# An attention and expert block on one core: extra steps spread over 24 score units, row maxima split after their transpose

## What is computed

```python
A1 = jnp.einsum('bhqd,bhkd->bhqk', Q1, K1) * scaling
A2 = jnp.einsum('bhqd,bhkd->bhqk', Q2, K2) * scaling
...
attn = jax.nn.softmax(A1, -1) - lam * jax.nn.softmax(A2, -1)
O = jnp.einsum('bhqk,bhkd->bhqd', attn, V)
rms = jnp.sqrt(jnp.mean(O * O, -1, keepdims=True) + EPS)
O = O / rms * rms_scale * (1.0 - LAMBDA_INIT)
...
logits = jnp.einsum('bth,eh->bte', x, router_w) + router_b
topv, topi = jax.lax.top_k(logits, TOP_K)
```

## Time and profile before

| | us |
|---|---|
| median of 3 runs | 1679.91 |
| lowest and highest | 1677.23, 1682.10 |
| the profiled execution | 1678.91 |
| its span | 1677.1 |

### The profile page before, as it was taken

The page is one execution under the profiler, slowest core; times in us unless marked ns, Lnnn a source line. Parts: engine busy times, 40 slices in busy tenths (PEclk is TensorE's granted clock), DMA queues, the critical chain, the costliest instruction groups (busy, mean ns, idle before and its releaser), DMA issues. The chain is left out here.

```text
span 1677.1 us, 44178 instructions
## 1 busy us (share of the span) xinstructions
PE 1340.8 (80%) x14048; PEld 940.4 (56%) x14049; DVE 1228.7 (73%) x3090; ACT 859.4 (51%) x1918; POOL 857.3 (51%) x1283
## 2 busy tenths in 40 slices
PE   1578888888888888888888888885199999999960
PEld 0345555555555555555555555553178888888850
DVE  3467887888888888888888888876756666666647
ACT  1156667666766676667666766664123333333320
POOL 0135566666666666666666666665323333333334
PEclk9999989998999899989998999896589999999985
DMA  5453444344434443444344434410111111111129
GB/s 203 99 111 76 112 109 101 86 111 109 105 85 108 112 105 84 111 111 105 83 111 111 106 83 108 105 39 17 43 44 44 44 44 46 43 44 45 44 76 296
DMA packets 182624, 151.73 MB, mean 90 GB/s; under 512 B 29555, under 2 KB 165369, under 8 KB 182068
## 3 DMA queue, kind: packets, MB, share of 16 engines
q1 hardware_dynamic: 165124, 122.11, 30.2%
q0 software_dynamic: 8448, 16.93, 3.3%
q10 hardware_dynamic: 8880, 10.49, 1.8%
HBM read 88.26 MB, written 60.51 MB: 89 GB/s over the span
## 5 line engine op out<-in xcount | busy, mean ns | idle before, releaser
L1190 DVE TENSOR_REDUCE mx<-p_max 128x2 f32<-128x512 f32 (+1 forms) x768 | 504.9, 685 | 198.3 <-PE p_max L816 188.9
L1009 ACT ACTIVATE probs<-p_exp 128x512 f32<-128x512 f32 x768 | 440.4, 601 | 239.7 <-PE p_exp L837 150.9
L1430 POOL TENSOR_SCALAR_AFFINE_SELECT probs<-probs 128x256 f32<-128x256 f32 (+1 forms) x768 | 366.3, 486 | 344.6 <-ACT probs L1009 333.3
L866 PE MATMUL p_out<-probs,v 128*32 128x256 f32 (+1 forms) x4096 | 253.3, 371 | 42.1 <-ACT ot L1000 35.7
L659 POOL DMA_INDIRECT pair_out<-on,v x136 | 133.7, 983 | 282.4 <-ACT on L569 274.6
L808 PE MATMUL p_max<-kt,qt 50*128 50x256 bf16 x1024 | 199.3, 293 | 35.6 <-ACT probs L1009 19.0
L866 PEld LDWEIGHTS p_out<-probs,v 128*32 128x32 f32 x4096 | 124.0, 119 | 145.2 <-POOL probs L1430 67.9
L837 PE MATMUL p_exp<-qt,kt 52*128 52x256 bf16 x1024 | 205.2, 289 | 0.0
L816 PE MATMUL p_max<-tri,ids 64*128 64x128 bf16 (+1 forms) x768 | 188.7, 253 | 0.0
L633 DVE TENSOR_TENSOR ot<-ot,p_max 128x512 f32<-128x512 f32 x136 | 93.5, 688 | 123.6 <-PE p_max L520 105.0
L816 PE MATMUL p_max<-tri,idb 64*128 64x128 bf16 (+1 forms) x768 | 172.3, 252 | 0.0
(11 more groups left out here) (174 smaller groups left out, 2750.5 us busy)
## 6 DMA issues: line engine op xcount, KB each, us to landing
qt<-q_parts SPq DMA_DIRECT2D x128, 192.0 KB
q_parts<-part_h SPq DMA_DIRECT2D x96, 128.0 KB, 1.9
kt<-k_parts SPq DMA_DIRECT2D x128, 96.0 KB
v<-rows_sorted SPq DMA_DIRECT2D x136, 65.0 KB, 1.8
q_parts<-part_m SPq DMA_DIRECT2D x64, 128.0 KB, 1.9
kt<-k_parts SPq DMA_DIRECT2D x128, 64.0 KB
qt<-pair_out SPq DMA_DIRECT2D x32, 256.0 KB, 5.0
mods<-mod_rows SPq DMA_DIRECT2D x32, 192.0 KB
```

Of the source, the lines that this page charges most:

```text
L866: m = nc.tensor.matmul(p_out[32 * j:32 * j + 32, pair, SEQ - n:SEQ], v[:, b.par, tile, 2 * g + head, :], src, start=(tile == 0), stop=(til ...
L1009: nc.scalar.activation(probs[:, quad % 2, k, :], p_exp[:, n % 3, :], ACT.Exp, scale=SCALE).then_inc(exp_done.sem, 1)
L1190: V.reduce_max(mx[:, w, tile, t, heads[0]:heads[-1] + 1], p_max[:, bank, :].rearrange("p (h k) -> p h k", h=len(heads)), AX.X, negate=True ...
L1430: G.affine_select(out=blocks, in_=blocks, compare_op=ALU.is_ge, fill=zero, base=0, pattern=[[0, count], [1, P]], channel_multiplier=-1).th ...
```

## The change

Every `body` is written over the 24 score units u, one unit a step, and the extra steps are spread over them anew. On DVE each unit's extra work stands right behind that unit's maximum. Where the main pieces stand, by the number of the score unit that they follow on their engine (b: before, a: after):

| piece | engine | b | a |
|---|---|---|---|
| outputs of groups 6, 7 (bC), 0 to 5 (b2) | PE | 0, 3, 6, 9, 12, 15, 18, 21 | 0, 2, 6, 8, 12, 14, 18, 20 |
| `xn` transposed | PE | 0 | 1 |
| first, second projection | PE | 2, 5 | 3, 7 |
| `low_part` 0, 1 | POOL | 6, 9 | 7, 11 |
| `ot` to rows, bC | PE | 8, 9 | 10, 13 |
| `ot` to rows, b2 | PE | 20, 21 | 17, 19 |
| logits | PE | 11 | 11 |
| values | PE | 12 | 15 |
| maxima of half 0 to rows | PE | 14 | 13 |
| rank products (`both`) | PE | 15 | 16 |
| `o`, `osq` | POOL | 12, 14 | 15, 16 |
| Newton steps 1 and 2; 3 and 4 | DVE | 21 | 22; 23 |
| `xn`, `h2` scaled | ACT | 23 | 0, 1 of the next iteration |

The maxima go another way. `take_max` writes them in the order that the rows need; PE transposes the fp32 columns of `mx` and no longer bf16 columns; ACT copies the rows and rounds them to bf16 (the high part, `nmt[:, 0]`); and the new DVE step `low_shift` subtracts that from the fp32 rows in PSUM (the low part, `nmt[:, 1]`). `minus_max`, `nm` and the semaphore `nm_step` go. The row numbers of the experts are converted to float by a copy where a multiplication by one did it (`topf`). SP's list is the same, but for the rows that `move_max` reads.

```diff
                     for part in range(SHIFTS):
-                        row, at = HU * NT * (t * SHIFTS + part), LANE * t + SHIFT_AT + part
+                        row, at = HU * NT * t, LANE * t + SHIFT_AT + part
                         sp.dma_start(qt[at:at + 1, 2 * b.par + w, :, :].rearrange("p h (l k) -> p (h l) k", l=NT),
-                                     nmt[row:row + HU * NT, w, :]).then_inc(nm_loaded[w].sem, 16)
+                                     nmt[row:row + HU * NT, part, w, :]).then_inc(nm_loaded[w].sem, 16)
...
-                wait(pe, nm_step, b, SHIFTS * (w + 1))
+                wait(pe, max_done, b, NBANKS // 2 * (w + 1))
                 settle(pe)
-                nc.tensor.transpose(p_mix[:, 1, 0:LANE].bitcast(BF16), nm[:, w, :], idb[:]).then_inc(nm_ps.sem, 1)
+                nc.tensor.transpose(p_mix[:, 1, 0:P], mx[:, w, :], idf[:]).then_inc(nm_ps.sem, 1)
...
-                for s in range(NH):
-                    n = s + s // 2
-                    scores(b1, b2, n)
-                    if s % 2:
-                        scores(b1, b2, n + 1)
-                    if s % 2 == 0:
-                        g = s // 2 - 2
-                        if g >= 0 and active(b2):
-                            outputs(b2, g)
-                        if g < 0 and active(bC):
-                            outputs(bC, g + PAIRS)
...
+                for u in range(NBANKS):
+                    scores(b1, b2, u)
+                    if u in (0, 2) and active(bC):
+                        outputs(bC, PAIRS - 2 + u // 2)
+                    if u in (6, 8, 12, 14, 18, 20) and active(b2):
+                        outputs(b2, 2 * (u // 6 - 1) + u % 6 // 2)
+                    if u == 1 and active(b2):
                         max_to_rows(i, b2, 1, 0)
-                    if s == 2 and active(bW):
...
-                    if s == 1 and active(bA):
...
+                    if u == 3 and active(bA):
                         wait(pe, ht_ready, bA)
                         project(i, bA, 0, 1)
-                    if s == 3 and active(bW):
-                        mix_free(pe, i, 1, 2)
+                    if u == 9 and active(bW):
...
-                    if s == 3 and active(bA):
-                        project(i, bA, 1, 2)
-                    if s == 5 and active(bC):
-                        outputs_to_rows(i, bC, 1, 0, 1, 4)
-                    if s == 6 and active(bC):
-                        outputs_to_rows(i, bC, 1, 1, 0, 3)
-                    if s == 4 and active(bR):
-                        mix_free(pe, i, 1, 3)
+                    if u == 7 and active(bR):
+                        mix_free(pe, i, 1, 2)
                         wait(pe, h2_step, bR)
...
-                        mix_free(pe, i, 1, 5)
+                    if u == 7 and active(bA):
+                        project(i, bA, 1, 2)
+                    if u == 11 and active(bR):
+                        mix_free(pe, i, 1, 4)
...
-                    if s == 8 and active(bV):
-                        mix_free(pe, i, 0, 4)
+                    if u == 10 and active(bC):
+                        outputs_to_rows(i, bC, 1, 0, 0, 3)
+                    if u == 13 and active(b1):
+                        max_to_rows(i, b1, 0, 5)
+                    if u == 13 and active(bC):
+                        outputs_to_rows(i, bC, 1, 1, 0, 4)
+                    if u == 15 and active(bV):
+                        mix_free(pe, i, 0, 5)
...
-                    if s == 9 and active(b1):
-                        max_to_rows(i, b1, 0, 6)
-                    if s == 10 and active(bR):
-
-                        mix_free(pe, i, 1, 7)
+                    if u == 16 and active(bR):
+
+                        mix_free(pe, i, 1, 6)
...
-                    if s == 13 and active(b2):
-                        outputs_to_rows(i, b2, 0, 0, 0, 5)
-                    if s == 14 and active(b2):
-                        outputs_to_rows(i, b2, 0, 1, 1, 8)
+                    if u == 17 and active(b2):
+                        outputs_to_rows(i, b2, 0, 0, 0, 6)
+                    if u == 19 and active(b2):
+                        outputs_to_rows(i, b2, 0, 1, 1, 7)
...
-                nc.scalar.copy(nmt[:, w, :], p_mix[0:NM_COLS, 1, 0:LANE].bitcast(BF16)).then_inc(nmt_ready.sem, 1)
+                nc.scalar.copy(nmt[:, 0, w, :], p_mix[0:MX_COLS, 1, 0:P]).then_inc(nm_high.sem, 1)
...
-                    wait(dve, nm_step, b.plus(-1), SHIFTS * (w + 1))
-                V.reduce_max(mx[:, w, tile, t, heads[0]:heads[-1] + 1],
+                    wait(dve, nm_ps, b.plus(-1), w + 1)
+                by_head = mx[:, w, 0:MX_COLS].rearrange("p (t h a) -> p t h a", t=2, h=HU)
+                V.reduce_max(by_head[:, t, heads[0]:heads[-1] + 1, tile],
...
-            def minus_max(b, w, k):
-
-                src = mx[:, w].rearrange("p a t h -> p t h a")
-                parts = nm[:, w, 0:NM_COLS].rearrange("p (t s h a) -> p t s h a", t=2, s=SHIFTS, h=HU)
-                if k == 0:
-                    wait(dve, max_done, b, NBANKS // 2 * (w + 1))
-                    wait(dve, nm_ps, b.plus(-1), w + 1)
-                    ins = V.tensor_scalar(parts[:, :, 0], src, ones_col[:, 0:1], None, ALU.mult)
-                else:
-                    wait(dve, nm_step, b, SHIFTS * w + 1)
-                    ins = V.tensor_tensor(parts[:, :, 1], src, parts[:, :, 0], ALU.subtract)
-                ins.then_inc(nm_step.sem, 1)
+            def low_shift(b, w):
+
+                wait(dve, nm_high, b, w + 1)
+                wait(dve, nm_loaded[w], b.plus(-1))
+                V.tensor_tensor(nmt[:, 1, w, :], p_mix[0:MX_COLS, 1, 0:P], nmt[:, 0, w, :],
+                                ALU.subtract).then_inc(nmt_ready.sem, 1)
...
+                        V.tensor_copy(topf[:].rearrange("p j t -> p t j"), top8i[:, :, 0:2]).then_inc(route.sem, 1)
-                            V.tensor_scalar(topf[:].rearrange("p j t -> p t j"), top8i[:, :, 0:2], ones_col[:, 0:1], None,
-                                            ALU.mult).then_inc(route.sem, 1)
...
+                    if u == 22:
+                        inverse_roots(i, [1, 2])
+                    if u == 23:
+                        inverse_roots(i, [3, 4])
...
-                    if active(b1) and s % 2:
-                        take_max(b1, n + 1)
...
-                for s in range(NH):
+                for u in range(NBANKS):
                     if active(b2):
-                        mask_bank(b2, s + s // 2)
-                        if s % 2:
-                            mask_bank(b2, s + s // 2 + 1)
-                    if s == 5 and active(bW):
...
-                    if s in (4, 6) and active(bA):
-                        low_part(bA, (s - 4) // 2)
-                    if s == 0 and active(bR):
...
+                        mask_bank(b2, u)
+                    if u == 2 and active(bR):
...
+                    if u in (7, 11) and active(bA):
+                        low_part(bA, (u - 7) // 4)
+                    if u == 13 and active(bW):
...
-                    if s in (12, 13, 14, 15) and active(bR):
-
-                        k = s - 12
+                    for k in {21: (0,), 22: (1, 2), 23: (3,)}.get(u, ()):
+                        if not active(bR):
```

277 lines of the change are left out of this document (134 added, 143 removed).

## The result

| | before | after |
|---|---|---|
| median | 1681.01 us (4 runs) | 1719.58 us (4 runs) |
| lowest and highest | 1677.23, 1684.34 | 1706.85, 1728.98 |
| the profiled execution | 1678.91 | 1728.98 |
| its span | 1677.1 | 1727.2 |

The changed kernel takes 1.0225 times the time of before (95% interval 1.0154 to 1.0297): slower, as forecast, but by 38.6 us where 6 to 8 were forecast, and 7.6 us above the range. The profiled executions of experiments 2 and 14 were disturbed (over 1.5% above the fastest of their kernel): the ratios leave them out and I explain no time from their traces, but the medians count them (without them 1630.58 and 1670.82 us).

What follows compares the result with a forecast made beforehand. Bound: unit 0 waiting for DMA loads behind `low_part`, 17.0 + 1.7 + 15.2 = 33.9 us a period. Steady +5, early +6, last -3 on 1678.9 gave 1687 us, range 1622 to 1712.

Steps and rivals of the forecast that it cites:

- the price of the clock's fall: PE's clock drops to 0.50 before the steps leading to `low_part`, delaying it 1.7 us a steady period (0 to 3.4).
- What bounds: Claim that PE's unit 0 waits for DMA `kt<-k_parts`, a loop through DMA from `low_part`'s end; period 33.9 us.
- The end of `low_part`, 18.7 us: The second `low_part` on POOL ends 17.0 us behind unit 0 at full clock, plus 1.7 for the clock's fall.
- The string, 15.2 us: SP's stores, moves and loads from the end of the second `low_part` to the next unit 0: 15.2 us.
- Four early periods, +6: Loop's first four periods, already waiting for loads: two more units ahead of `low_part`, 1.5 us each, +6 us.
- The last iteration, -3: Last period has no loads to wait for and keeps the gain of removed PE stalls: -3 us.
- What the change takes away: DVE loses 3.4 us a period, gains about 0.6; spreading ends most PE stalls, 2 to 3 us a period.
- Full clock: Rival: loads bind but PE's clock doesn't fall before the first half; period 32.2, 1642 us (1612 to 1650); chance 0.17.
- Slower still: Rival: POOL's `o` beside DVE's `chosen` and `both` delays `low_shift`, lengthening SP's string; 35 us a period, 1717; chance 0.12.
- The spreading doesn't do what it says: Rival: PE still waits at unit 16 for `both`, up to 1.1 us under the DMA string; no separate chance.
- The engines bind: Rival: with earlier `low_part` or shorter SP string, DVE, PE and handshakes give 30 us a period, 1580 us; chance 0.09.

Runs made afterwards that it cites:

- experiment 2: Changed kernel with SP's six query stores waiting for the first `low_part` alone: 1634.42 us, 0.9718 of before.
- experiment 14: Changed kernel with query parts stored early and POOL's scatters of sorted rows moved behind units 3 to 6 of the next iteration: 1671.63 us, 0.9931 of before.
- experiment 1: Changed kernel with seven unread products (results nobody reads) on PE behind units 21 to 23: 1627.52 us, 0.9706 of before.
- experiment 3: Kernel before with SP's six query stores waiting for the first `low_part` alone: 1669.94 us, 0.9956 of before.
- experiment 9: Kernel before, its order kept, with the new path of the maxima alone, `low_shift` of half 0 between `max_index` and `topf`: 1681.08 us, 1.0 of before.
- experiment 17: Changed kernel with four unread products, query parts stored early and scatters moved behind units 3 to 6 of the next iteration: 1587.01 us, 0.9447 of before.
- experiment 12: Changed kernel with query parts stored early and four unread products, scatters left behind units 21 to 23: 1680.28 us, 0.9998 of before.
- experiment 13: Changed kernel with seven unread products, query parts stored early and scatters moved behind units 3 to 6 of the next iteration: 1614.65 us, 0.9641 of before.
- experiment 5: Changed kernel with seven unread products and query parts stored early, scatters left behind units 21 to 23: 1654.54 us, 0.9835 of before.
- experiment 7: Changed kernel's order alone, with the maxima as in before (`minus_max` at units 0 and 12): 1725.11 us, 1.0228 of before.
- experiment 10: Changed kernel with the chain to the second `low_part` one unit earlier: 1716.43 us, 1.0216 of before.
- experiment 11: Changed kernel with the chain to the second `low_part` one unit earlier and query parts stored early: 1689.66 us, 1.0049 of before.
- experiment 8: Kernel before with five unread products on PE, three behind unit 15 and two behind units 16 and 17: 1651.73 us, 0.982 of before.

## Why the prediction was right in its direction and wrong in size

**The step that failed** is the price of the clock's fall. The prediction put it at 1.7 us in a steady period and at nothing in the four early periods and in the last iteration. Experiment 1 is the same order with the clock held up: against it the kernel after is longer by 2.9 us in a steady period (34.48 against 31.62), by 7 us in the four early periods together and by 18 us in the last iteration. The forecast missed the profiled execution by 42 us, of which 16 are steady, 10 early and 16 at the end.

**What bounds.** Right. In the kernel after unit 0 waits for DMA `kt<-k_parts`; experiments 1, 2 and 3 move the two terms apart and the time follows each.

**The end of `low_part`, 18.7 us.** Nearly right in sum, by luck, since two errors cancel: it ends 18.9 us behind unit 0 on average. At full clock it is 16.3 (experiment 1), not 17.0, and the fall of the clock costs 2.6, not 1.7. The one early period from which I took 1.7 was too mild a sample: I said nothing to 3.4 us and took the 1.7 that it showed, while the joint of after gives PE up to 10.2 us at 0.50.

**The string, 15.2 us.** It was 15.5 on average. The two shortfalls, 0.2 and 0.3 us, are nearly all of the 0.6 a period by which the steady part is over the forecast (34.48 against 33.9), 16 us in 27 periods.

**Four early periods, +6.** It was +16. The second period alone went from 29.2 to 37.0 us. One product of unit 6 there, and the same kind at full clock in the middle:

```profile
103.08 0.42 PE L814 MATMUL p_max<-tri,idb 64*128 64x256 bf16 x1
...
568.35 0.27 PE L814 MATMUL p_max<-tri,idb 64*128 64x256 bf16 x1
```

0.42 us is what such a product takes in a stretch at 0.50. The trace has no record of the clock before 107.7 us, so the 1.00 that a window reads there is no measurement; by the products' own durations PE is at the lower level from the loop's start to that moment, and `low_part` ends 20.8 us behind unit 0. In before this lasts to 94.7 us. I had priced two units more ahead of `low_part` and left the clock out of these periods, where the earlier trace rows had shown it falling. A part of this term is chance: over the twelve traces of the new order that I read the moment lies between 93 and 119 us, and the second period between 29.6 and 38.3 us, longest where it comes last.

**The last iteration, -3.** Wrong in sign: +13. I priced the stalls that go and took the clock as in before. Experiment 1 gives the same iteration 53 us in place of 71 with the same instructions and the clock at 1.00. So this term is the clock as well. Over after's four runs the time spreads by 22 us, over before's by 7; which term spreads isn't shown, as one of the four has a trace.

**What the change takes away.** DVE's work in a steady period fell by 1.6 us (748.44 less 705.49 over 27), not 2.8. `low_shift` is 0.27 us a piece, a good estimate. But the 1.04 us of `topf` were not its conversion. In experiment 9 the copy takes 0.26 us, and `chosen` behind it 0.99, where before `topf` 1.04 was followed by a short `chosen`: what is slow is the one of these steps that meets POOL's `osq`. None of it mattered, since DVE wasn't in the bound.

**The rivals.** *Full clock* was priced at 1642, 1612 to 1650; experiment 1 makes it true and gives 1627.5. *Slower still*: its mechanism is there, beside another step. POOL's `o` and DVE's `both` in after:

```profile
600.14 1.28 POOL L1444 TENSOR_TENSOR o<-on 128x512 f32<-128x512 f32 x1
...
600.24 1.21 DVE L1335 TENSOR_TENSOR both<-chosen 128x16 bf16<-128x16 f32 x1
```

`both` ends with `o`; it took 0.17 to 0.30 us elsewhere. `low_shift` stands ahead of `o` and isn't touched, so nothing reached SP, and 1717 was near the result for another reason. The Trainium skill's GPSIMD Engine Reference, section Key points, has DVE instructions with two SBUF inputs contend with GpSimd for its interfaces; these rows agree. *The spreading doesn't do what it says*: true for `both` (0.8 us a period, 1.12 before) and hidden under the string, as said. *The engines bind*, 1580: needed a shorter string and a full clock, and with both, and the scatters moved (experiment 17), the time is 1587. PE is the fullest engine there, busy 785.47 of 826.19 us, and taking unread products from it made the kernel faster. The Trainium skill's Perfetto Trace Analysis, section Identifying the Most-Contended Engine, would have one optimise the engine with the highest occupancy first; the kernel before contradicted that and this one agrees, as far as busy time tells, which the same section doesn't count as a good measure for TensorE.

**What stays open.** Why results come late where scatters lie at the joint. That they depend on the scatters is shown: with the scatters moved it is gone in every period (17 against 12 on one chip, 13 against 5 on two). But the kernel after and experiments 1 and 2 show none of it with the scatters in the same place: in 1 and in 5 the fourth scatter starts 1.5 us behind unit 0, and unit 1's maximum starts at 2.0 in 1 and at 3.2 in 5. Here the chip is a rival that no run tests. Experiments 1 and 2 ran on the first chip; the five that show late results (5, 7, 10, 11, 12) ran on the other two. In these five unit 1's maximum never starts less than 1.48 us behind the start of the fourth scatter, in 135 steady periods; in 1 it does so in all 27, in 2 in 25, and in the kernel after in 3 (in the others unit 1 itself comes later). So 5 may owe its place behind 1 and 2 to its chip and not to the two edits meeting; the chip of the kernel after isn't on record.

## What to carry to other kernels

Before spreading work over a loop, find the loop that closes through DMA and ask when its first step ends; stalls removed behind that step turn into one long wait, and the wait takes TensorE's clock with it. A fall of the clock belongs to whatever stands behind the wait, so price it in the early and last iterations too, and measure it by giving the engine harmless work in the wait. Compare two orders with the clock held up in both before you call one the worse. A step of 0.3 us placed 3 us later can cost as much as a whole change, if a bank or a queue hangs on it.

## What the runs showed of the hardware

- Unread products made a kernel faster: 7 of them gave 92 us of 1720 (experiment 1; 87 by the ratios), 5 gave 30 us in the kernel before (experiment 8).
- In experiments 5, 7, 10, 11 and 12, all on two of the three chips, the results of PE's next unit came up to 2.8 us late while POOL issued indirect scatters, with no wait in PE's records: 1.3 us in 5, 2.4 to 2.6 in most periods of 12. In 1 and 2, on the third chip, they came in time. Moving the scatters took unit 1's maximum on DVE from 4.4 to 2.0 us behind unit 0 (12 against 17, one chip).
- A DVE step of 128x16 with two inputs beside a 1.28 us POOL step took 1.21 us in place of 0.17 to 0.30.
- The trace's record of the granted clock begins at 107.7 us in after and 94.7 in before; a window ahead of it reads 1.00 whatever the clock. In after PE's products there take the durations that they have at 0.50 (0.42 us in place of 0.27):

```profile
103.00:108.00 5.00, 5.00 (x39) 2.57 (x38) 1.38 (x2) 1.67 (x3) 2.16 (x3) 1.00 0.00 2
```
